# A four-round graph kernel: TensorE's signals in the edge stages move from the last matmul of a group to a drain behind it

## The reference

```python
h = relu(layernorm(x))
m1 = segment_sum(h[src], dst) / deg            # round 0
m2 = segment_sum(m1[src], dst) / deg           # round 1
x = x + 0.5 * m1 + 0.5 * m2
h = relu(layernorm(x))
def conv(h, W_msg, W_edge, W_root, b):
    msg = h[src] @ W_msg + edge_attr @ W_edge
    agg = segment_max(msg, dst)                # 0 for a node without edges
    return leaky_relu(agg + h @ W_root + b)
out = x + conv(conv(h, W1...), W2...)          # rounds 2 and 3
```

## Time and profile before

| | |
|---|---|
| median of 3 timed runs | 9666.22 us (9662.51 to 9667.9) |
| the profiled execution | 9629.93 us, span 9628.2 us |
| edge stage of round 0 | 61 to 2331 us |
| edge stage of round 1 | 2413 to 4666 us |
| edge stage of round 2 | 4788 to 7111 us |
| edge stage of round 3 | 7225 to 9549 us |
| busy PE, DVE, ACT, POOL | 58%, 34%, 16%, 67% of the span |
| mean granted TensorE clock | 0.648 of full speed |

### The profile page before, as it was taken

The page is one execution under the profiler, slowest core; times in us unless marked ns, Lnnn a source line. Parts: engine busy times, 40 slices in busy tenths (PEclk is TensorE's granted clock), DMA queues, the critical chain, the costliest instruction groups (busy, mean ns, idle before and its releaser), DMA issues.

```text
span 9628.2 us, 100471 instructions
## 1 busy us (share of the span) xinstructions
PE 5576.1 (58%) x25651; PEld 4095.6 (43%) x25651; DVE 3262.5 (34%) x6693; ACT 1500.7 (16%) x5073; POOL 6458.6 (67%) x6525
## 2 busy tenths in 40 slices
PE   2333333334233333333578877878887887887888
PEld 1222222223222222222555555555564555555556
DVE  4333333334333232323423333333332333333334
ACT  1000000001000000000322222222232222222223
POOL 5666666664666666666566666766656666666665
PEclk6555555556555555555767777777786777677776
DMA  3111111111111111111133333333323333333332
GB/s 79 35 34 34 34 34 34 34 35 39 47 35 34 34 34 35 34 34 35 46 76 77 77 77 77 78 80 78 77 64 71 80 78 77 77 77 77 77 81 64
DMA packets 309643, 548.56 MB, mean 57 GB/s; under 512 B 183464, under 2 KB 183464, under 8 KB 284712
## 3 DMA queue, kind: packets, MB, share of 16 engines
q0 software_dynamic: 200192, 307.90, 16.3%
q1 hardware_dynamic: 108804, 239.50, 9.7%
q10 hardware_dynamic: 548, 0.17, 0.0%
HBM read 522.27 MB, written 24.87 MB: 57 GB/s over the span
## 4 chain that ended last, share of the span: by engine, by line
another core or an unknown queue 29%; PE 26%; issue 9%; DVE 8%; DVEq 2%; ACT 1%; ACTq 1%; POOL 0%; DMA 0%; POOLq 0%; SPq 0%
PE ps L578 7%; PE ps L576 6%; PE ps L600 6%; PE ps L589 3%; DVE arena L799 3%; DVE comp L784 3%; PE ps L557 2%; DVE arena L767 2%; DVEq L257 1%; DVEq L784 1%; PE ps L662 1%; PE ps L638 0%; ACTq L257 0%; PE ps L675 0%
## 5 line engine op out<-in xcount | busy, mean ns | idle before, releaser
L374 POOL DMA_INDIRECT rows<-table,src_sb x6256 | 6273.4, 1003 | 2930.3 <-issue 1767.5
L557 PE MATMUL ps<-arena,rows 128*98 128x128 f32 (+1 forms) x6256 | 1418.1, 399 | 2967.0 <-DVE comp L784 2634.6
L557 PEld LDWEIGHTS ps<-arena,rows 128*98 128x98 f32 (+1 forms) x6256 | 1179.5, 254 | 3226.7 <-DVE comp L784 2836.3
L799 DVE TENSOR_TENSOR_SCAN arena<-arena,ps 96x512 f32<-96x512 f32 x782 | 996.6, 1274 | 3238.6 <-remote 1989.8
L784 DVE TENSOR_TENSOR comp<-comp,ps 98x128 f32 (+1 forms) x3128 | 893.6, 286 | 2878.4 <-remote 2317.0
L578 PEld LDWEIGHTS ps<-ident,rows 128*96 128x96 f32 x6256 | 950.4, 208 | 912.9 <-issue 912.7
L600 PE MATMUL ps<-arena 128*96 128x128 f32 x6256 | 1180.2, 352 | 108.6 <-issue 72.4
L578 PE MATMUL ps<-ident,rows 128*96 128x128 f32 x6256 | 1173.3, 344 | 54.2 <-issue 53.4
L576 PE MATMUL ps<-arena,we 32*96 32x512 f32 x1564 | 1143.7, 819 | 27.3 <-DMA rows<-table,src_sb 27.3
L600 PEld LDWEIGHTS ps<-arena 128*96 128x96 f32 x6256 | 1052.2, 228 | 129.6 <-issue 124.4
L767 DVE TENSOR_TENSOR arena<-iota_b,meta 128x512 f32<-128x512 bf16 x1564 | 1053.0, 673 | 59.6 <-issue 55.1
(11 more groups left out here) (84 smaller groups left out, 1026.0 us busy)
## 6 DMA issues: line engine op xcount, KB each, us to landing
arena<-flags SPq DMA_DIRECT2D x194, 768.0 KB
rows<-table,src_sb POOLq DMA_INDIRECT x6256
arena<-in_eat SPq DMA_DIRECT2D x194, 256.0 KB
table<-arena SPq DMA_DIRECT2D x56, 336.0 KB, 2.7
out<-xs SPq DMA_DIRECT2D x13, 336.0 KB
xs<-in_x SPq DMA_DIRECT2D x6, 672.0 KB, 5.9
arena<-flags SPq DMA_DIRECT2D x2, 576.0 KB
src_sb<-in_srcs SPq DMA_DIRECT2D x1, 782.0 KB, 5.2
```

The lines of the kernel that those rows point to most:

```text
L374: pool.indirect_dma_start(rows[:, g % RING, j, 0:D], None, tables[r][:, :], bass.IndirectOffsetOnAxis(src_sb[:, c:c + 1], 0)).then_inc(lan ...
L557: m = pe.matmul(ps[0:w, at + k * P:at + (k + 1) * P], rows[:, j, k, 0:w], hot[:, j % HOTS, k, :], start=True, stop=True)
L799: dve.tensor_tensor_scan(run[:, slot % SCANS], fe[0:D, slot // UNIT, q * W:(q + 1) * W], ps[0:D, ROWS + slot % 2 * BANK:ROWS + slot % 2 * ...
```

## The change

Five signals move from the last matmul of their group of matmuls to a drain that follows it in TensorE's queue: `picked` and `counted` in `sum_windows`, `rows_ps` in `rows_of`, `runT_ps` in `back`, `picked` in `pick`. The drain is an instruction of TensorE's sequencer. Nothing else is different: the matmuls, their order, the waits and the other engines' code stay. Per group there are two drains in round 0, one in round 1 and three in rounds 2 and 3, which is 391 x (2 + 1 + 3 + 3) = 3,519 in all.

```diff
                         for k in range(GRP):
-                            m = pe.matmul(ps[0:w, at + k * P:at + (k + 1) * P], rows[:, j, k, 0:w], hot[:, j % HOTS, k, :],
-                                          start=True, stop=True)
-                        m.then_inc(picked[r], 1)
+                            pe.matmul(ps[0:w, at + k * P:at + (k + 1) * P], rows[:, j, k, 0:w], hot[:, j % HOTS, k, :],
+                                      start=True, stop=True)
+                        pe.drain().then_inc(picked[r], 1)
...
-                                      start=(known(g) and g == 0), stop=last, skip_group_check=True).then_inc(counted, 1)
+                                      start=(known(g) and g == 0), stop=last, skip_group_check=True)
+                            pe.drain().then_inc(counted, 1)
...
                     for k in range(GRP):
-                        m = pe.matmul(ps[0:D, at + k * P:at + (k + 1) * P], rows[:, slot, k, 0:D], ident[:, :],
+                        pe.matmul(ps[0:D, at + k * P:at + (k + 1) * P], rows[:, slot, k, 0:D], ident[:, :],
                                       start=False, stop=(k == GRP - 1))
-                    m.then_inc(rows_ps[r], 1)
+                    pe.drain().then_inc(rows_ps[r], 1)
...
-                        m = pe.transpose(ps[:, at:at + D], run[:, slot % SCANS, k * P:(k + 1) * P], ident[0:D, 0:D])
-                    m.then_inc(runT_ps[r], 1)
+                        pe.transpose(ps[:, at:at + D], run[:, slot % SCANS, k * P:(k + 1) * P], ident[0:D, 0:D])
+                    pe.drain().then_inc(runT_ps[r], 1)
...
-                        m = pe.matmul(ps[0:D, at:at + P], runT[:, slot % SCANS, k, :], hot[:, slot % HOTS, k, :],
+                        pe.matmul(ps[0:D, at:at + P], runT[:, slot % SCANS, k, :], hot[:, slot % HOTS, k, :],
                                       start=True, stop=True)
-                    m.then_inc(picked[r], 1)
+                    pe.drain().then_inc(picked[r], 1)
```

## The result

The changed kernel takes 11,151.85 us (median of 4 runs, 11,151.03 to 11,158.37), the kernel before, measured beside it, 9,664.36 us (4 runs, 9,656.97 to 9,667.9). The ratio is 1.1542 with a 95% interval of 1.1523 to 1.156: slower, by 1,487 us. The forecast was 11,250 us.

The account below looks back on a forecast made before the run. No engine plainly bound the kernel: POOL's pace plus held TensorE signals did; with drains, half-clock TensorE would bound the maxima. 9630 + 1494 (maxima) + 140 (sums) = 11,264, say 11,250 us; range 9,700 to 12,100.

Parts of the forecast that it names:

- 7.85 us a group: Rounds 2 and 3: TensorE at the half clock with three drains, 6.24 + 1.6 us a group, +747 us each round.
- the prediction's first term: Rounds 2 and 3: a drain forbids overlap of one stage's last matmul with the next's first, 0.49 us a group.
- three other terms of the prediction: Rounds 2 and 3, per group: drain ends 0.15 us, sequencer work and first weight load 0.75, uncovered weight loads 0.2.
- holes of 0.4 to 0.5 us: Sign in the timeline of rounds 2 and 3: TensorE idle that long behind L578, L589 and L600.
- the hold: All edge stages: TensorE's signals are held back while POOL issues without a pause; 1008 us of POOL's idleness.
- what the prediction expected of POOL's pauses: Rounds 2 and 3: POOL idles some 2.6 us a group, which should keep signals from being held; nothing added.
- self-locking half clock: Rounds 2 and 3: at the half clock TensorE is behind POOL, every group has three holes, so the clock stays half.
- faster rival: Rounds 2 and 3: full clock despite holes, over half the time, TensorE hidden behind POOL; 8,590 or 9,100 us; chance 0.18.
- +70 a round, +140: Rounds 0 and 1, the sums: the drain's signal stays held and TensorE no longer computes the next group meanwhile; 0.18 us a group.
- the rival with the escaping drain: Drain signals escape the hold, sums gain 520 us, but TensorE bounds rounds 2 and 3: 10,600 us; chance 0.30.
- one POOL pause of 3.5 us in every fourth group instead of every fifth: Rounds 0 and 1: the assumed pause frequency behind the sums' loss, 0.18 us a group.
- the prediction's 8,590: Faster case's total in us, with all edge stages at POOL's pace, 5.1 us a group in sums and 5.3 in maxima.

Follow-up runs that it names:

- r2_after: The changed kernel with all drains, unedited, run again on the second chip: 10,553.18 us, ratio 1.2379 to the kernel before; maxima stages 3041 us each.
- e1: Changed kernel with the two drains of the sums undone, the three in the maxima kept: 10,546.44 us, ratio 1.2378 to the kernel before.
- e2: Changed kernel with all five drains kept but signalling nothing, every increment back on its matmul: 10,517.58 us, ratio 1.2345 to the kernel before.
- e9: Changed kernel with all drains, but the maxima leave out the edge part's matmuls and half of pick's products: 8,484.15 us, ratio 0.996 to the kernel before.
- e3: Kernel before plus one drain a group in the maxima, behind `rows_of`: 8,937.41 us, ratio 1.0476 to the kernel before.
- e7: Kernel before plus two drains a group in the maxima, behind `rows_of` and `pick`: 8,550.66 us, ratio 1.0039 to the kernel before.
- e4: Kernel before without drains; in the maxima TensorE waits for its own signal behind `rows_of`, `back` and `pick`: 10,070.26 us, ratio 1.1813 to the kernel before.

## Why the prediction was right, and where it was not

**Right: TensorE bounds the maxima.** The step said 7.85 us a group. Measured: 3,073 and 3,072 us a stage, +748 and +747, 7.86 us a group. A group inside the stage takes 7.71 us, and its parts can be read off: 0.88 us of holes (0.33 + 0.32 + 0.23), 0.49 us of overlap lost (the prediction's first term, from the earlier trace rows) and 0.1 us for L601's eight, 2.02 us in place of 1.92: 6.24 + 1.47 = 7.71. The three other terms of the prediction were 0.15 + 0.75 + 0.2 = 1.1 us and measure 0.98. The last of them was misread: the earlier trace rows have L578's eight at 2.02 us without a pause before them, and the drains left them there; only `pick`'s eight grew by 0.1 us. The timeline was to show holes of 0.4 to 0.5 us; they are 0.23 to 0.33.

The 0.15 us between 7.71 and the stage's mean of 7.86 was in no step, and the trace shows its two parts. One is the loop: in every eighth group, where it turns, the hole before the first matmul is about 0.8 us and not 0.23, which is 0.07 us a group. The other is the hold. At the start of each maxima stage, while POOL fills its empty ring without a pause, one group takes 38 to 39 us:

```profile
4829.21 2.02 PE L579 MATMUL ps<-ident,rows 128*96 128x128 f32 x8
4839.60 0.90 PE L590 MATMUL ps<-ident,arena 96*128 96x96 f32 x4 [8.37 <-issue]
4848.21 1.99 PE L601 MATMUL ps<-arena 128*96 128x128 f32 x8 [7.71 <-issue]
4860.44 0.94 POOL L374 DMA_INDIRECT rows<-table,src_sb  x1 [0.30 <-issue]
4866.44 1.98 PE L577 MATMUL ps<-arena,we 32*96 32x512 f32 x2 [16.24 <-issue]
```

That is 31 us a stage, and just what the stages take more than r2_after's 3041. Behind it POOL waits once a group and no group takes over 8.5 us, so what the prediction expected of POOL's pauses came, but for this start. That the total fits to 3 us a stage is partly luck: the terms were 0.12 us too high and 0.15 us was missing. e1 shows that the drains of the maxima alone carry the loss, e2 that it is not the signal's sender, and e9 that the loss is gone when the group fits under POOL's pace.

**Right for three drains, wrong as a rule: the self-locking half clock.** The clock was 0.50 throughout, and POOL idled 2.6 us a group (2029.6 / 782), as forecast. But the reason given, that the clock is full "only where TensorE ran without a hole", fell. In e3 and e7 it rises while nearly every group has its hole of 0.22 to 0.36 us, and in e7 a second of 0.23 us. The faster rival's mechanism (the clock up in spite of holes, TensorE hidden behind POOL) is what two drains did; its condition, full for over half of the time, was met there at 0.56. What brings the clock back sooner with two drains than with one, and never with three, was not found. It is not the length of the holes: e4's 0.06, 0.13 and 0.06 us are shorter in sum than e3's one, and the clock stayed at half. Before each rise that was looked at, TensorE had been at it for groups on end with its drain holes alone, and so it had where no rise came. This stays open.

**Mis-sized: the sums.** The step "+70 a round, +140" measured +19 and +12, together +31. The direction was right: a drain doesn't escape the hold. In the group shown the signal came 1021.64 - 1014.70 = 6.9 us late and the fold 7.5 (the prediction named 10 to 18; the longest such drain lasted 21.5 us), and the release came 3.3 us after POOL's last gather, as before (3.4). So the rival with the escaping drain (10,600 us) fell. What failed is the term "one POOL pause of 3.5 us in every fourth group instead of every fifth", which had no row behind it. The waits of the sums alone (61 to 4666 us before, 61 to 4697 after) show what it should have been:

```profile
POOL rows L374 <- remote: 522.9, 172, 5.8
POOL rows L374 <- PEq L559: 580.3, 257, 6.8
```

POOL's pauses became more frequent, one in 3.0 of the 782 groups instead of one in 4.5, but shorter, 2.3 us instead of 3.0. Together they grew by 57 us, not 140. POOL's 0.3 us gaps ("issue", 899.5 us before, 880.2 after) and its busy time in these stages (1536 + 1534 before, 1568 + 1494 after) gave back 27 of these, which leaves 30 of the 31. That TensorE makes up after each release what it no longer does before it is a likely reason for the shorter pauses, and not shown.

**The sum.** The forecast was +1,634 us; measured by spans it is 11,150 - 9,628 = +1,522, of which the maxima are +1,495 and the sums +31, and the rest of the kernel took 4 us less. With the sums at +31, the forecast would have been 9,630 + 1,494 + 31 = 11,155.

**Not settled: the hold.** The prediction reads the earlier trace rows as signals held while POOL issues. The experiments' three chips run the same program without them, at 8,520 us, 70 us under the prediction's 8,590 for stages at POOL's pace. So the price of the hold was read well enough (1,140 us, by the prediction 9,630 - 8,590 = 1,040), but its cause was not found: whether it goes by the chip, by where the data lie or by something else could not be tried, since no experiment met it. In particular it isn't shown that POOL's issuing holds the signals; the rows show only that they come 3 to 5 us after POOL stops. A drain does nothing against it, which the first comparison shows by itself.

The Trainium skill, page "PSUM — Partial Sum Buffer", section "Engine vs sequencer instructions", advises the increment on the matmul and a drain only as a stand-alone barrier. It gives this as a rule of correctness and names no price. The runs bear the advice out on time as well: three stops a group cost 0.5 us each in TensorE's time, and the signal gained nothing. The Trainium skill's page "TensorE: Matmul & The Clock Gate", part "NX overlap", gives 219 cycles over its columns for a lone matmul, which is 183 ns at the half clock, by which the prediction estimated 0.55 us a group. The measured price is 1.47 us, made of the lost overlap (0.49), the holes that the timeline puts down to issue (0.88) and 0.1 for L601.
